# Shifted attention: four score products at once, in four row quarters and four banks, with the bias added by VectorE for every head group

## The reference, cut to what matters

```
attn = jnp.einsum('whqd,whkd->whqk', q * scale, k)      # 64 windows, 8 heads of width 8, 128 x 128
rpb  = bias_table[rel_idx]                              # per head, 128 x 128
attn = attn + jnp.transpose(rpb, (2, 0, 1))[None]
attn = jax.nn.softmax(attn, axis=-1)
out  = jnp.einsum('whqk,whkd->wqhd', attn, v)
```

## Time and profile before

| what | us |
|---|---|
| median of 3 runs | 1288.12 (1284.66 to 1289.18) |
| profiled execution, its own time | 1284.39 |
| its span, first to last instruction | 1282.5 |
| TensorE busy | 1169.3 (91% of the span) |
| VectorE busy | 854.3 (67%) |
| ScalarE busy | 754.3 (59%) |
| GpSimd busy | 621.2 (48%) |

### The profile page before, as it was taken

The page is one execution under the profiler, slowest core; times in us unless marked ns, Lnnn a source line. Parts: engine busy times, 40 slices in busy tenths (PEclk is TensorE's granted clock), DMA queues, the critical chain, the costliest instruction groups (busy, mean ns, idle before and its releaser), DMA issues.

```text
span 1282.5 us, 43492 instructions
## 1 busy us (share of the span) xinstructions
PE 1169.3 (91%) x16198; PEld 804.4 (63%) x16198; DVE 854.3 (67%) x2765; ACT 754.3 (59%) x2435; POOL 621.2 (48%) x939
## 2 busy tenths in 40 slices
PE   6988889999999979999999998899999999789997
PEld 3446745555555547777777777677777764457665
DVE  5964667777777766887877876655555555746664
ACT  0136758888888855555555444566666666544553
POOL 6012456767676752565555654433333332245555
PEclk9989999999999989999999999999999999889999
DMA  6000000000000000000000000000000000000000
GB/s 227 1 1 2 2 1 2 0 0 0 0 0 0 0 2 2 2 0 0 0 0 0 0 0 2 2 1 0 0 0 0 0 1 1 1 2 19 16 17 17
DMA packets 10833, 10.26 MB, mean 8 GB/s; under 512 B 9232, under 2 KB 9872, under 8 KB 10640
## 3 DMA queue, kind: packets, MB, share of 16 engines
q1 hardware_dynamic: 10768, 9.35, 2.5%
HBM read 7.25 MB, written 2.10 MB: 7 GB/s over the span
## 4 chain that ended last, share of the span: by engine, by line
PE 56%; issue 15%; DVE 10%; POOL 10%; ACT 6%; POOLq 1%; DMA 0%; SPq 0%; ACTq 0%; DVEq 0%
PE bank L1405 8%; POOL big L573 7%; PE bank L1753 5%; PE bank L1771 5%; PE bank L1400 4%; PE bank L1088 3%; PE bank L1388 3%; PE bank L159 3%; PE bank L1115 2%; PE bank L1518 2%; PE bank L1156 2%; PE bank L1080 2%; PE bank L1166 2%; PE bank L1107 2%; DVE big L1253 1%
## 5 line engine op out<-in xcount | busy, mean ns | idle before, releaser
L573 POOL TENSOR_TENSOR big<-big 128x512 f32<-128x512 f32 x128 | 133.0, 1039 | 57.5 <-DVE big L774 57.5
L743 ACT ACTIVATE big<-big 128x128 f32<-128x128 f32 x384 | 148.9, 394 | 0.4 <-DVE big L786 0.4
L994 POOL TENSOR_TENSOR big<-big 128x512 f32<-128x512 f32 x64 | 65.6, 1045 | 118.6 <-DVE big L1264 118.6
L1486 POOL TENSOR_TENSOR big<-g_a,g_b 64x64 f32 x128 | 40.1, 313 | 171.0 <-DVE g_a L1476 171.0
L1467 DVE TENSOR_TENSOR_SCAN g_t<-g_zero_r,bank 128x128 f32<-128x128 f32 x128 | 53.8, 420 | 86.6 <-ACT g_zero_r L1452 86.6
L680 PEld LDWEIGHTS bank<-cst,big 128*128 128x128 f32 x512 | 56.3, 140 | 73.2 <-issue 58.5
L1674 POOL TENSOR_TENSOR big<-big 128x512 f32<-128x512 f32 x48 | 61.0, 1270 | 72.7 <-DVE big L1877 70.1
L1807 ACT ACTIVATE big<-bank 128x512 f32<-128x512 f32 x128 | 66.1, 604 | 48.5 <-PE bank L1753 48.5
L786 DVE CUSTOM_DVE_ANT_0 big<-bank,cst 128x128 f32<-128x128 f32 x384 | 88.3, 286 | 9.3 <-issue 9.3
L1452 ACT ACTIVATE g_zero_r<-bank,g_bias 128x64 f32<-128x64 f32 x128 | 40.7, 318 | 88.3 <-PE bank L1405 88.2
L634 PE MATMUL bank<-big 32*128 32x512 f32 x256 | 75.0, 637 | 15.5 <-POOL big L567 8.0
(11 more groups left out here) (275 smaller groups left out, 3228.1 us busy)
## 6 DMA issues: line engine op xcount, KB each, us to landing
cst<-consts_dram SPq DMA_DIRECT2D x1, 3364.5 KB, 14.6
out_dram<-h SPq DMA_DIRECT2D x8, 256.0 KB, 2.6
big<-x_dram SPq DMA_DIRECT2D x3, 512.0 KB, 6.2
cst<-consts_dram SPq DMA_DIRECT2D x3, 256.0 KB
big<-x_dram SPq DMA_DIRECT2D x1, 513.0 KB, 4.6
big<-consts_dram SPq DMA_DIRECT2D x4, 96.0 KB, 2.1
cst<-consts_dram SPq DMA_DIRECT2D x4, 48.0 KB, 2.0
g_ih_exchanged<-consts_dram SPq DMA_DIRECT2D x2, 96.0 KB, 7.6
```

The costliest lines, as they stand in the source:

```text
L573: nc.gpsimd.tensor_tensor(P, P, a_rs[t % 4].unsqueeze(2).to_broadcast([128, 4, 128]), ALU.mult).then_inc(a_n_r, 1)
L743: m = nc.scalar.activation(P, raw, ACT.Exp, bias=a_mx[tb % 4][:, k:k + 1], scale=-1.0, accum_out=a_sm[tb % 4][:, k:k + 1])
L994: nc.gpsimd.tensor_tensor(w, w, f_rs[l][:, 8 * s:8 * s + 8].unsqueeze(2).to_broadcast([128, 8, 64]), ALU.mult).then_inc(f_w_r, 1)
```

## The change

`scores(i, l)` now issues a pair's four score products in one go, at the head of slot u = 0, each in its own row quarter and bank and each with its own increment of `a_sc_r`. It waits once, for the queries, the spread keys and all four minima of the pair before. The bias product is gone; VectorE adds the bias for u = 3 as for the others (memset, four custom instructions), into `a_P`, and ScalarE's exponentials of u = 3 read `a_P` in SBUF. The wait for the earlier transposes of that buffer moves from ScalarE to VectorE. The text of `spread` is unchanged. The two scores ahead of the loop are gone.

```diff
--- before.py
+++ after.py
@@ -619,25 +619,15 @@
             nc.tensor.matmul(bank(3)[:, 0:128], c("a_k"), xT[l], start=True, stop=True)
             nc.tensor.matmul(bank(2)[:, 256:384], xT[l], c("a_v"), start=True, stop=True).then_inc(a_qkv_r, 1)
 
-        def scores(i, t):
-            l, u = t // 4, t % 4
-            if u == 0:
-                pe.wait_ge(a_q_r, i * 2 + (l + 1))
-                pe.wait_ge(a_kz_r, i * 2 + (l + 1))
-            if t >= 4 or exists(i, -1):
-
-                if u == 3:
-                    pe.wait_ge(a_e_r, i * 8 + (t - 3))
-                else:
-                    pe.wait_ge(a_mx_r, i * 8 + (t - 3))
-            r = slice(32 * u, 32 * u + 32)
-            m = nc.tensor.matmul(scores_bank(t), a_q[l][r, :], a_kz[l][r, :], start=True, stop=u != 3)
-            if u != 3:
-                m.then_inc(a_sc_r, 1)
-
-        def bias(t):
-
-            nc.tensor.matmul(scores_bank(t), eye, c("a_bias", 512, 1024), start=False, stop=True).then_inc(a_sc_r, 1)
+        def scores(i, l):
+
+            pe.wait_ge(a_q_r, i * 2 + (l + 1))
+            pe.wait_ge(a_kz_r, i * 2 + (l + 1))
+            if l or exists(i, -1):
+                pe.wait_ge(a_mx_r, i * 8 + 4 * l)
+            for u in range(4):
+                r = slice(32 * u, 32 * u + 32)
+                nc.tensor.matmul(scores_bank(u), a_q[l][r, :], a_kz[l][r, :], start=True, stop=True).then_inc(a_sc_r, 1)
 
         def attended(i, t):
             l, u = t // 4, t % 4
@@ -669,6 +659,8 @@
 
         def slot(i, t):
             l, u = t // 4, t % 4
+            if u == 0 and exists(i, 0):
+                scores(i, l)
             ib, tb = back(i, t, 3)
             if exists(ib, 0):
                 pe.wait_ge(a_n_r, ib * 8 + (tb + 1))
@@ -684,12 +676,6 @@
                 attended(ib, tb)
             if u == 1 and exists(i, l, N2 - 1):
                 qkv(i + l, 1 - l)
-            if t % 2:
-                for d in (1, 2):
-                    if exists(i, (t + d) // 8):
-                        scores(i + (t + d) // 8, (t + d) % 8)
-            if u == 2 and exists(i, 0):
-                bias(t + 1)
             if u == 0:
                 if exists(i, l, N2 - 1):
                     rows(i + l, 1 - l)
@@ -710,8 +696,6 @@
 
         pe.wait_ge(f_dve, SETUP3)
         pe.wait_ge(m_loaded, LOADED7)
-        scores(0, 0)
-        scores(0, 1)
         pipelined(pe, slot)
 
     def stage2_act(act):
@@ -735,12 +719,9 @@
             ib, tb = back(i, t, 1)
             if exists(ib, 0):
                 act.wait_ge(a_mx_r, ib * 8 + (tb + 1))
-                if tb % 4 == 3 and (tb >= 4 or exists(ib, -1)):
-                    act.wait_ge(a_pt_r, ib * 8 + (tb - 3))
                 for k in range(4):
                     P = a_P[tb % 4][:, 128 * k:128 * (k + 1)]
-                    raw = scores_bank(tb)[:, 128 * k:128 * (k + 1)] if tb % 4 == 3 else P
-                    m = nc.scalar.activation(P, raw, ACT.Exp, bias=a_mx[tb % 4][:, k:k + 1], scale=-1.0, accum_out=a_sm[tb % 4][:, k:k + 1])
+                    m = nc.scalar.activation(P, P, ACT.Exp, bias=a_mx[tb % 4][:, k:k + 1], scale=-1.0, accum_out=a_sm[tb % 4][:, k:k + 1])
                 m.then_inc(a_e_r, 1)
             ib, tb = back(i, t, 3)
             if tb % 2 and exists(ib, 0):
@@ -775,14 +756,10 @@
             if exists(i, 0):
 
                 v.wait_ge(a_sc_r, i * 8 + (t + 1))
-                if u != 3 and (t >= 4 or exists(i, -1)):
+                if t >= 4 or exists(i, -1):
                     v.wait_ge(a_pt_r, i * 8 + (t - 3))
-
-                if u == 3:
-                    m = nc.vector.tensor_reduce(a_mx[t % 4], scores_bank(t).rearrange("p (j k) -> p j k", j=4), X, ALU.min)
-                else:
-                    nc.vector.memset(spare[:, 24 + t:25 + t], 0.0)
-                for k in range(0 if u == 3 else 4):
+                nc.vector.memset(spare[:, 24 + t:25 + t], 0.0)
+                for k in range(4):
                     m = nc.vector.tensor_tensor_reduce(a_P[t % 4][:, 128 * k:128 * (k + 1)], scores_bank(t)[:, 128 * k:128 * (k + 1)],
                                                        c("a_bias", 512 * (u % 2) + 128 * k, 512 * (u % 2) + 128 * (k + 1)), 1.0, 3e38,
                                                        ALU.add, ALU.min, a_mx[t % 4][:, k:k + 1])
```

## The result

| | us |
|---|---|
| before, median of 8 runs | 1287.22 (1284.27 to 1289.18) |
| changed, median of 8 runs | 1282.85 (1277.93 to 1284.07) |
| ratio | 0.9962, 95% interval 0.9944 to 0.998 |
| changed, profiled execution | 1283.67, span 1281.8, mean granted clock 0.953 (before 0.976) |

The change gains 4.4 us. The forecast was 1259, a gain of 29 us, with a range of 1247 to 1277, so the time lies above the range: the kernel gained too little.

What follows compares the result with a forecast made beforehand. TensorE's order set the pace at 9.16 us a pair, ScalarE next; a period of 8.15 saves 28.3 us over 28 pairs, plus 0.7 elsewhere: 29 us, 1255.4 as profiled, 1259 as median, range 1247 to 1277.

Steps and rivals of the forecast that it cites:

- no longer the bound by work: TensorE in stage 2: its work per pair was to fall to 6.6 us, below ScalarE's 8.15.
- rival (d): TensorE's clock falls in the new pauses; with half of 28 pairs at 1.2 GHz, 42 us slower, 1330; chance 0.06.
- S of four: TensorE's step of four score products at the head of a pair, taken at 1.06 us.
- Rival (a): The row quarters go only two by two, the score step costs 2.12 us; no change, 1284 to 1288; chance 0.07.
- The period at full clock: Time per pair in stage 2, taken as ScalarE's busy time, 8.15 us, against 9.16 before.
- The long loop: From the second exponentials' end through minima, scores, transposes, qkv and queries to the next second exponentials; 8.04 us.
- The pair with the centring: Every other pair, where centring and a reduction add 0.97 us to VectorE's loop of 7.2, making 8.1.
- Free: GpSimd in stage 2: no work added, 6.5 us a pair, with the scores `spread` waits for done earlier.
- rival (b): Waits behind the single score step compound to 8.6 us a pair; saving 16 us, 1272; chance 0.18.
- the loops: Chains of waits between engines through the new score step; each had to stay under ScalarE's 8.15 us.
- the stretch from 468 to 472: Earlier profile: clock stayed at 1.00 with TensorE busy 1.95 of 4 us, falling only in the next stretch.
- that from 84 to 88: Earlier profile: clock fell to 0.62 with TensorE busy 2.92 of 4 us, read as having no long pause.

Runs made afterwards that it cites:

- e1: The changed kernel with two unused products of 256 columns put into TensorE's pause before the transposes of slot u = 3: 1259.06 us.
- e7: The changed kernel with the three qkv products issued ahead of the product with the values, no filler: 1254.22 us.
- e4: The changed kernel with one unused product of 128 columns in TensorE's pause before the transposes of slot u = 3: 1269.89 us.
- e9: The kernel before without bias product, VectorE adding all four biases, scores still two at a time, qkv ahead of the product with the values: 1254.79 us.
- e11: A repeat of e7, the changed kernel with qkv ahead of the product with the values: 1252.73 us.
- e10: The kernel before with only the qkv products moved ahead of the product with the values: 1283.24 us.

## Why the prediction was wrong

The step that failed is the clock. The sum took all of TensorE's work at a clock of 1.00 ("no longer the bound by work"), put the cost of falls at nothing and left them to rival (d) with 6%. Measured: the clock fell in 14 of 29 pairs, at 1.39 us each. Of the 25 us of gain that are missing, 19.5 are these and some 4 the full period. The rest of the sum held, or nearly:

- S of four was taken at 1.06; measured 1.07. Rival (a) is out. The Trainium skill's 3.07 times ("TensorE: Matmul & The Clock Gate", "Measured speedup vs the span model") does not fit here: four products in 1.07 against 0.96 for one of the same width is 3.6 times.
- The period at full clock was taken at 8.15; measured 8.28. The long loop, 8.04 on paper, is 8.13. The pair with the centring is 8.43, by a path that no sum of the prediction has: centring, reciprocal, normalisation, `spread`, S, with GpSimd in it, which was "Free". This is rival (b) in small: 0.13 us a pair, 4 us.
- With the clock held (e1) the kernel takes 1259.06. By its ratio that is 2.2% or 28 us less than before, against 29 forecast. In its profile the stage takes 271.9 us where it took 298.4. To the microsecond it is luck, as the loops cost 4 us more than I reckoned.

The clock was missed in two places. First, I read the earlier trace rows as speaking both ways and gave the stretch from 468 to 472 as much weight as that from 84 to 88. The first is a single stretch, followed by a fall. And of the other I said that TensorE "had no long pause there". Its rows in the kernel before say that pauses of nearly 1 us stand just ahead of the fall, which began at 85.0:

```profile
83.33 0.66 PE L349 MATMUL bank<-xc,wqk 128*64 128x128 f32 x8 [0.95 <-DVE big L433]
84.76 0.65 PE L369 MATMUL bank<-big 32*128 32x128 f32 x8 [0.77 <-DVE f_bout_diagonal L901]
```

They come again every 4 to 5 us (0.86 us twice, then 1.00, up to 97.4), and from 88 to 100 us the clock is 0.50. That was the row to trust: the attention was about to get such a pattern.

Secondly, I had the pauses in hand (0.5 to 1.5 us, every pair), and they came out a little longer (1.45 to 1.74), but I gave the clock one all-or-nothing price. It isn't so: a fall here hits the head of one pair and costs 1.39 us over a full pair, not the 5.0 that (d) has (13.2 less 8.15). So it was wrong as well that the clock decides from 20% of the pairs on: 14 of 29 pairs fell, and the kernel was still faster. With the price of a fall from the slow rows, half of the pairs would have given 29 - 14 x 1.4 = 9 us, 1279; that price was only known afterwards.

The Trainium skill, "TensorE: Matmul & The Clock Gate", under "HAM oscillation — how this bites in real kernels", tells of a kernel whose clock falls again and again in its waits, and advises to restructure the loop so that TensorE stays fed. The remedy holds here: e7 reorders the loop, and 2 of 31 pairs fall in place of 15. The waits differ: there they are for transfers and longer, here pauses of 1.45 to 1.74 us behind GpSimd and ScalarE did it in half of the pairs.

What stays open: why the same pause is followed by a fall in one pair and not in the next, why a pause of 1.3 us mostly spares the clock in e7 and in e4 but not always, and why it stayed low for 12.5 us in e9. The runs show how often it happened, not by what rule.

## What to carry to other kernels

Work that is taken off the engine that sets the pace turns into pauses of that engine; on TensorE ask at once where they will lie and what runs right behind them, since the low clock lands there. Look then for a step in the new critical loop that can be issued earlier: here the same 0.36 us of reordering gave 5 us in the kernel before and 29 in the changed one, 1254 against 1283. And try each half of a change alone. Here the bias moved to VectorE carries all of the gain (1264.12 alone). The four scores at once, without it, made the kernel 140 us slower; together with it they cost 19 us, until qkv was moved, and then they were worth nothing (1254.22 against 1254.79).

## What the runs showed of the hardware

- Two fp32 products of 256 columns that nobody reads, in TensorE's pause, made the kernel 24 us faster (1282.85 to 1259.06); the same two at the head of the pair made it 30 us slower (1312.63).
- The granted clock fell to 0.50 right behind pauses of 1.45 to 1.74 us of TensorE, in 14 of 29 pairs that all had such a pause. In e7, e11 and e4, where the pauses are 1.0 and 1.3 us in turn, it fell in 1, 2 and 5 of 29 pairs (the first two left out), always behind the 1.3; behind 0.4 to 0.7 us, in e1, in none. In another stage of the kernel before it fell behind 0.95 and 0.77 us.
- Four fp32 products of 32 rows by 512 columns in four row quarters and banks took 1.07 us, two took 1.06.
- The same steps of TensorE in another order (A, T, qkv, A for A, T, A, qkv) took 1.97 us in place of 2.17 (e10).
